# Loading the first image's shifted rows inside SBUF, in a convolution, attention and expert kernel

## What is computed

```python
xn = (x - mean) * rsqrt(var + 1e-5) * ln_g + ln_b          # mean, var over the whole image
Q, K, V = depthwise3x3(per_head_1x1(xn))                   # 8 heads of 24 channels
attn = softmax(K^T Q / alpha)                              # 24 x 24 per head, over channels
x = w_f (V attn) + b_f + xn
t = tokens(x)                                              # 1024 tokens of 192
t = t + proj(proj(causal_attention(layernorm(t))))         # 6 heads of 32; the projection is applied twice
t = t + experts(layernorm(t), top 2 of 4)                  # gelu, 192 -> 768 -> 192
```

## Time and profile before

| | us |
|---|---|
| median of 3 runs | 3337.73 |
| lowest and highest run | 3334.97, 3342.5 |
| span of the profiled execution | 3332.3 |
| TensorE busy | 3067.4 (92%) |
| first convolution round begins | 43.44 |
| fifth round (last pair's) begins | 79.19 |

### The profile page before, as it was taken

How to read it: one execution, slowest core, us unless ns; L and a number is a source line. 1 busy time by engine, 2 the same in 40 slices (tenths; PEclk the granted TensorE clock), 3 DMA queues, 4 the chain that set the end, 5 groups by cost and what they waited for, 6 DMA issues and landing times. The chain is left out here.

```text
span 3332.3 us, 72396 instructions
## 1 busy us (share of the span) xinstructions
PE 3067.4 (92%) x26642; PEld 2344.2 (70%) x26642; DVE 2202.3 (66%) x5619; ACT 1871.5 (56%) x3996; POOL 874.5 (26%) x1142
## 2 busy tenths in 40 slices
PE   4999999999999999999999999958999999999995
PEld 1666667666666676666766766637888888888884
DVE  3777677677776776777767767664555655655653
ACT  0647456465474664654746647535555555555553
POOL 2121313303223133132230331450223223223222
PEclk9999999999999999999999999979999999999997
DMA  7546445454364454544644546515667767667673
GB/s 177 142 114 178 115 124 148 124 150 126 113 184 116 122 149 122 153 118 120 173 125 115 148 123 154 156 47 159 195 206 213 221 208 220 210 205 228 206 212 120
DMA packets 256516, 519.82 MB, mean 156 GB/s; under 512 B 70919, under 2 KB 161991, under 8 KB 246521
## 3 DMA queue, kind: packets, MB, share of 16 engines
q1 hardware_dynamic: 222878, 453.58, 48.6%
q0 software_dynamic: 29184, 59.81, 6.0%
q10 hardware_dynamic: 4107, 1.81, 0.3%
HBM read 242.82 MB, written 117.71 MB: 108 GB/s over the span
## 5 line engine op out<-in xcount | busy, mean ns | idle before, releaser
L1051 DVE TENSOR_REDUCE minus_max<-ps 128x1 f32<-128x128 f32 (+7 forms) x768 | 571.6, 750 | 243.7 <-PE ps L1772 232.3
L1469 ACT ACTIVATE p_sb<-ps,minus_max 128x128 f32<-128x128 f32 (+7 forms) x768 | 569.3, 741 | 41.3 <-DVE minus_max L1051 37.8
L1782 PE MATMUL ps<-ident,p_sb 128*128 128x128 f32 x3456 | 530.6, 279 | 44.2 <-ACT p_sb L1469 18.4
L1356 DVE TENSOR_TENSOR g_lo<-g,g_hi 128x512 fp32r<-128x512 f32 x402 | 282.8, 704 | 369.3 <-ACT g_hi L1593 369.3
L1592 ACT ACTIVATE g<-ps,bcur 128x512 f32<-128x512 f32 x402 | 276.6, 688 | 429.2 <-PE ps L1967 429.2
L1483 ACT ACTIVATE PT<-ps 128x512 f32<-128x512 f32 (+3 forms) x768 | 396.7, 517 | 132.7 <-PE ps L1782 123.5
L1782 PEld LDWEIGHTS ps<-ident,p_sb 128*128 128x128 f32 x3456 | 370.0, 141 | 99.4 <-ACT p_sb L1469 37.5
L1983 PE MATMUL ps<-w_all,g_hi 128*128 x1608 | 434.6, 351 | 0.0
L1770 PE MATMUL ps<-KS,QS 96*128 96x512 f32 (+3 forms) x1152 | 393.6, 401 | 21.4 <-ACT p_sb L1469 17.9
L1647 PE MATMUL ps<-ring,wconv 125*32 125x512 f32 (+1 forms) x3072 | 358.4, 606 | 15.0 <-DMA ring<-padded_scratch 15.0
L780 POOL DMA_INDIRECT routed_rows<-xhat,slot x256 | 253.3, 989 | 358.2 <-issue 358.2
(11 more groups left out here) (276 smaller groups left out, 5442.5 us busy)
## 6 DMA issues: line engine op xcount, KB each, us to landing
ring<-padded_scratch SPq DMA_DIRECT2D x576, 204.0 KB
cur<-w_all SPq DMA_DIRECT2D x67, 1536.0 KB, 7.1
routed_rows<-zero_rows SPq DMA_DIRECT2D x67, 384.0 KB, 5.0
xgt<-routed_rows SPq DMA_DIRECT2D x67, 384.0 KB, 4.6
expert_rows<-y_rows SPq DMA_DIRECT2D x67, 384.0 KB, 3.0
padded_scratch<-xpad SPq DMA_DIRECT2D x32, 435.0 KB, 3.6
x_sb<-x SPq DMA_DIRECT2D x16, 768.0 KB, 5.5
KS<-QKh SPq DMA_DIRECT2D x128, 96.0 KB
```

Of the source, the lines that this page charges most:

```text
L1051: v.tensor_reduce(nmx[:, qc, h:h + 1], score_place(n), AX, ALU.max, negate=True).then_inc(mx_sb, 1)
L1356: v.tensor_tensor(g_lo[:, n % 2, :], g32[:, n % 2, :], g_hi[:, n % 2, :].bitcast(F32), ALU.subtract).then_inc(lo_sb, 1)
L1469: a.activation(p_sb[n % NP][:, 0:P * (qc + 1)], score_place(n), ACT.Exp, bias=nmx[:, qc, h:h + 1], accum_out=ls[:, qc, h:h + 1]).then_inc( ...
L1782: last = t.transpose(bank(pass_bank(piece))[:, P * k:P * (k + 1)], p_sb[n % NP][:, P * (k0 + k):P * (k0 + k + 1)], ident[:, :])
```

## The change

For the first image the ring is no longer filled through DRAM. `first_pair(sp, p)` waits for the half of xn that the pair lies in and issues 18 DMAs that copy 24 partitions each from `xpad` straight into `ring[p]`, so 72 DMAs of 102 KB in the place of two stores and 36 loads; SyncE issues the four pairs in order, right behind the mask rows. The semaphores `ring_ld[p]` count 288 for the first image and 144 for each later one. Before VectorE overwrites xpad for the second image it waits for the four pairs' copies, in the place of the stores. The seven gate loads go to ScalarE's queue, behind the projection's loads and ahead of the last small ones. TensorE runs `conv(0, 0)` first (after `setup_dve` 2, the product of L930), and the projection's products between `conv(0, 0)` and `conv(0, 1)`.

```diff
@@ -284,6 +284,7 @@
         setup_pool, inside_zero, mask_rows, setup_dve, setup_pe, w_split = sems(
             "setup_pool inside_zero mask_rows setup_dve setup_pe w_split")
         RING_LOADS = 16 * len(TAPS)
+        FIRST_LOADS = 2 * RING_LOADS
         STACK_LOADS = 16 * 3
         SENT = 16 * 2 * NC
 
@@ -324,6 +325,21 @@
                 sp.wait_ge(conv_ps, NR * i)
             sp.dma_start(x_sb[:, :, :], x[i].rearrange("(h p) a b -> p h (a b)", h=2)).then_inc(x_ld, 16)
 
+        def ring_loaded(i):
+
+            return FIRST_LOADS + RING_LOADS * i
+
+        def first_pair(queue, p):
+
+            half, at_row = p // 2, 2 * HC * (p % 2)
+            queue.wait_ge(xn_sb, half + 1)
+            for s, taps in enumerate(STACKS):
+                for j, tap in enumerate(taps):
+                    for h in range(2):
+                        rows = slice(at_row + HC * h, at_row + HC * (h + 1))
+                        queue.dma_start(ring[p][s][HC * j:HC * (j + 1), h, :],
+                                        xpad[rows, half, SHIFT[tap]:SHIFT[tap] + SL]).then_inc(ring_ld[p], 16)
+
         def write_scratch(sp, i, h):
 
             sp.wait_ge(xn_sb, 2 * i + h + 1)
@@ -331,7 +347,7 @@
 
         def load_pairs(sp, i, h):
 
-            sp.wait_ge(scr_w[h], 16 * (i + 1))
+            sp.wait_ge(scr_w[h], 16 * i)
             for p in (2 * h, 2 * h + 1):
                 for s, taps in enumerate(STACKS):
                     for j, tap in enumerate(taps):
@@ -510,17 +526,8 @@
                     sp.dma_start(ring[p][s][HC * nt:HC * nt + nt, :, :],
                                  inside_taps[taps[0]:taps[0] + nt, :].unsqueeze(1).to_broadcast([nt, 2, SL])
                                  ).then_inc(w_ld["mask"], 16)
-            write_scratch(sp, 0, 0)
-            load_pairs(sp, 0, 0)
-            write_scratch(sp, 0, 1)
-            sp.dma_start(gw_bc[:, 0:P, :], gate_w_a.partition_broadcast(P)).then_inc(w_ld["gate"], 16)
-            sp.dma_start(gw_bc[:, P:C, :], gate_w_b[0:CB, :].partition_broadcast(P)).then_inc(w_ld["gate"], 16)
-            sp.dma_start(bf_bc[:, 0:C], b_f.partition_broadcast(P)).then_inc(w_ld["gate"], 16)
-            sp.dma_start(gb_bc[:, :], gate_b.partition_broadcast(P)).then_inc(w_ld["gate"], 16)
-            sp.dma_start(gcol[:, :], gate_w_a[0:HALF, :]).then_inc(w_ld["gate"], 16)
-            sp.dma_start(ident_g[0:P - HALF, HALF:HALF + E], gate_w_a[HALF:P, :]).then_inc(w_ld["gate"], 16)
-            sp.dma_start(ident_g[P - HALF:HALF, HALF:HALF + E], gate_w_b[0:CB, :]).then_inc(w_ld["gate"], 16)
-            load_pairs(sp, 0, 1)
+            for p in range(PAIRS):
+                first_pair(sp, p)
             sp.dma_start(wqa_src[:, :], w_qkv_a).then_inc(w_ld["qkv"], 16)
             sp.dma_start(wqb_src[:, :], w_qkv_b).then_inc(w_ld["qkv"], 16)
             sp.wait_ge(setup_pool, 5)
@@ -905,8 +912,12 @@
                     if i:
 
                         dve.wait_ge(xn_flat, 2 * i)
+                        if i == 1:
+                            for p in range(PAIRS):
+                                dve.wait_ge(ring_ld[p], ring_loaded(0))
                         for h2 in range(2):
-                            dve.wait_ge(scr_w[h2], 16 * i)
+                            if i > 1:
+                                dve.wait_ge(scr_w[h2], 16 * (i - 1))
                 rows = lambda a: a.rearrange("p (a b) -> p a b", b=SW)
                 v.scalar_tensor_tensor(out=interior(h), in0=rows(x_sb[:, h, :]), scalar=img[:, 5:6],
                                        in1=rows(lnb[:, h, :]), op0=ALU.mult, op1=ALU.add).then_inc(xn_sb, 1)
@@ -1513,6 +1524,13 @@
             a.dma_start(bp_src[:, 0:1], b_proj[0:P].rearrange("(p a) -> p a", a=1)).then_inc(w_ld["proj"], 16)
             a.dma_start(bp_src[0:CB, 1:2], b_proj[P:C].rearrange("(p a) -> p a", a=1)).then_inc(w_ld["proj"], 16)
             a.dma_start(bpb[:, :], b_proj.partition_broadcast(P)).then_inc(w_ld["proj"], 16)
+            a.dma_start(gw_bc[:, 0:P, :], gate_w_a.partition_broadcast(P)).then_inc(w_ld["gate"], 16)
+            a.dma_start(gw_bc[:, P:C, :], gate_w_b[0:CB, :].partition_broadcast(P)).then_inc(w_ld["gate"], 16)
+            a.dma_start(bf_bc[:, 0:C], b_f.partition_broadcast(P)).then_inc(w_ld["gate"], 16)
+            a.dma_start(gb_bc[:, :], gate_b.partition_broadcast(P)).then_inc(w_ld["gate"], 16)
+            a.dma_start(gcol[:, :], gate_w_a[0:HALF, :]).then_inc(w_ld["gate"], 16)
+            a.dma_start(ident_g[0:P - HALF, HALF:HALF + E], gate_w_a[HALF:P, :]).then_inc(w_ld["gate"], 16)
+            a.dma_start(ident_g[P - HALF:HALF, HALF:HALF + E], gate_w_b[0:CB, :]).then_inc(w_ld["gate"], 16)
             for j in range(HPH):
                 a.dma_start(convb[W * j:W * j + HC, PAIRS:NR], conv_bias[2 * W:2 * W + HC, j:NH:HPH],
                             allow_slow_non_contiguous=True).then_inc(w_ld["small"], 16)
@@ -1612,25 +1630,14 @@
             pe.wait_ge(setup_pool, 2)
             average_mean(pe, 0, 4)
             average_var(pe, 0, 4)
-            pe.wait_ge(w_ld["proj"], 16 * 7)
-            pe.wait_ge(setup_dve, 4)
-            wa, wb, wta, wtb = wp_src[0], wp_src[1][0:CB, :], wp_src[2], wp_src[3][0:CB, :]
-            for b, rows, la, lb in ((5, P, wa[:, 0:P], wb[:, 0:P]), (6, CB, wa[:, P:C], wb[:, P:C]),
-                                    (7, P, bp_row[:, 0, :], bp_row[0:CB, 1, :])):
-                t.matmul(bank(b)[0:rows, 0:C], la, wta[:, :], start=True, stop=False, skip_group_check=True)
-                last = t.matmul(bank(b)[0:rows, 0:C], lb, wtb, start=False, stop=True, skip_group_check=True)
-                if rows == CB:
-                    t.matmul(bank(b)[CB:P, 0:C], la, wta[:, :], start=True, stop=False, skip_group_check=True)
-                    last = t.matmul(bank(b)[CB:P, 0:C], lb, wtb, start=False, stop=True, skip_group_check=True)
-            last.then_inc(setup_pe, 1)
-            pe.wait_ge(setup_dve, 4)
+            pe.wait_ge(setup_dve, 2)
             pe.wait_ge(w_ld["mask"], 16 * 2 * PAIRS)
             pe.wait_ge(img_veps, 1)
 
             def conv(i, r):
                 kind, n = ROUNDS[r]
                 if kind == "pair":
-                    pe.wait_ge(ring_ld[n], RING_LOADS * (i + 1))
+                    pe.wait_ge(ring_ld[n], ring_loaded(i))
                     tiles = [(2 * n + j % 2, W * (j // 2)) for j in range(4)]
                 else:
                     tiles = [(HPH * n + j, 2 * W) for j in range(4)]
@@ -1841,8 +1848,19 @@
                 t.matmul(o[:, E:2 * E], ones128[:, :], rowsum[:, :], start=True, stop=True, skip_group_check=True
                          ).then_inc(count_ps, 1)
 
-            for r in range(2):
-                conv(0, r)
+            conv(0, 0)
+            pe.wait_ge(w_ld["proj"], 16 * 7)
+            pe.wait_ge(setup_dve, 4)
+            wa, wb, wta, wtb = wp_src[0], wp_src[1][0:CB, :], wp_src[2], wp_src[3][0:CB, :]
+            for b, rows, la, lb in ((5, P, wa[:, 0:P], wb[:, 0:P]), (6, CB, wa[:, P:C], wb[:, P:C]),
+                                    (7, P, bp_row[:, 0, :], bp_row[0:CB, 1, :])):
+                t.matmul(bank(b)[0:rows, 0:C], la, wta[:, :], start=True, stop=False, skip_group_check=True)
+                last = t.matmul(bank(b)[0:rows, 0:C], lb, wtb, start=False, stop=True, skip_group_check=True)
+                if rows == CB:
+                    t.matmul(bank(b)[CB:P, 0:C], la, wta[:, :], start=True, stop=False, skip_group_check=True)
+                    last = t.matmul(bank(b)[CB:P, 0:C], lb, wtb, start=False, stop=True, skip_group_check=True)
+            last.then_inc(setup_pe, 1)
+            conv(0, 1)
             conv_transposes(0, 0)
             for i in range(B):
                 conv(i, 2)
```

## The result

The kernel with the change takes 3358.14 us (median of 7 runs, 3340.99 to 3369.21) against 3337.76 (7 runs, 3334.29 to 3342.5) of the kernel before: a ratio of 1.0052, with a 95% interval of 1.0037 to 1.0068. By the ratio it is slower by some 17 us; the two medians lie 20.4 us apart. The forecast was 3336 with a range of 3328 to 3345, so direction and range were both wrong. The profiled execution took 3360.47, with a span of 3358.6.

A forecast was written before the change was run, and what follows sets the result against it. TensorE, busy for 92% of the span, was taken as the bound, so only its start could move: 2 us off the span of 3332.3 gives 3330.3, plus 5.4 to the median gives 3336, range 3328 to 3345.

The forecast's parts named there:

- When the loads land: ScalarE's small loads in the first image's setup: `wf_t` expected at 50 to 58 us, hidden by the second pair.
- Late small loads: Rival: `wf_t` queued behind gate and projection loads beside the copies lands at 75, token rows at 107, 3345 us; chance 0.10.
- the prize: TensorE's 15.0 us of waiting for pairs; the waits on the store could give back some 8 us at most.
- The cost of an issue: SyncE's 72 copy issues at 0.43 us each, 7.8 us a pair, hidden under the 11.4 us transfer.
- The transfer: Copies inside SBUF filling the ring: 13.7 GB/s per busy engine, 0.317 us a row, 11.4 us a pair.
- The ratio of 1.22: A skill page's speedup of SBUF traffic over HBM traffic, giving 8.6 us a pair; the prediction said the trace disagrees.
- When they start: Copies issued at 18.95, held behind mask rows until about 26; pairs land at 41, 54, 65.6 and 77.2 us.
- The projection's products: TensorE's eight steps of 7.1 us, moved to 47.4 to 54.5, hidden by the second pair's wait but for 0.5 us.
- The rest: L930's product comes ten us before the first pair; VectorE's new wait and the dropped store wait cost or gain nothing.
- The sum's step: From the forecast span of 3330.3 to the median: 5.4 us added, giving 3335.7, say 3336.

The follow-up runs named there:

- e1: The kernel before with only the seven gate loads moved to ScalarE's queue, behind the projection's loads: 3341.03 us, ratio 1.0013.
- e6: The changed kernel with the last small loads (biases, alpha, `wf_t`) ahead of the projection's and gate's loads on ScalarE's queue: 3353.78 us, ratio 1.0054.
- e3: The changed kernel with SyncE holding the first copy until the projection's, gate and small loads have landed: 3353.24 us, ratio 1.0049.
- e4: The changed kernel with the projection's, gate, alpha and `wf_t` loads issued by SyncE ahead of the mask rows: 3336.82 us, ratio 0.9998.
- e7: The changed kernel with projection, alpha and `wf_t` loads early on SyncE, gate loads after pair 0, pairs 0 to 2 split between SyncE and ScalarE: 3341.47 us, 1.0014.
- e5: The kernel before with only the projection's products moved between the first and second convolution rounds: 3337.52 us, ratio 1.0002.
- e2: The kernel before with the SBUF copies alone, gate loads and projection's products left in their old places: 3349.39 us, ratio 1.0040.
- e9: The changed kernel with early projection, alpha and `wf_t` loads; SyncE copies pairs 0, 2, ScalarE pair 1 before its biases, pair 3 shared: 3347.67 us, 1.0025.

## Why the prediction was wrong

**When the loads land** is the step that failed, in the rival *Late small loads*. Its mechanism was the right one in kind; what was wrong was "I expect 50 to 58" and the chance of 0.10. The argument against it was "many small rows passed in between at the start (593 packets in 9 us)". That row was misread. Its window of the kernel before, 28 to 37, split where SyncE issues the first load of the ring, 28 to 28.86 and 28.86 to 37:

```profile
q10 hardware_dynamic: 297, 0.08, 45.7%
```

```profile
q1 hardware_dynamic: 348, 1.24, 67.6%
q10 hardware_dynamic: 296, 0.03, 3.9%
```

Half of the 593 packets passed in the first 0.86 us, before any load of the ring was issued. The other 296 took 8.1 us beside 348 of SyncE's; on 16 engines that is one per 0.44 us. This was already the slow turn-taking, and slower than the changed kernel's (546 in 10 us, one per 0.29). The rows of `wf_t`, which the prediction has "at nearly one for one", came slower than that: while they passed, from 38 to 44, ScalarE's queue passed 231 packets to 423 of SyncE's.

What had saved the loads before was the stretch just ahead, in which SyncE waited for its store and 1506 packets passed. The prediction read that wait as the prize. For ScalarE's loads it was the quiet in which they landed, and no step asked who else used it. One part the rival didn't have at all: it counted rows that wait in the queue, and 23.8 of the 33.3 us were lost earlier, in ScalarE's issuing. The gate loads alone account for 4.7 of these (e1 issues `wf_t` at 36.81).

The prediction said that "the projection's loads (another 44) have no quiet gap", but priced only `wf_t`. The products wait for these loads: 57.5 in place of the 47.4 at which they were put, and this alone moved the second round's end from 60.4 to 70.9. So a `wf_t` at 58 would not have saved the forecast: in e6 ScalarE is ready at 53.5, and the first transposes still begin at 77.7. And "from there to 99.84 it has about 30 us of work" was right as busy time (24.27 and 5.71 us from 78 to 124) but left out VectorE's waits: from its first piece to the token rows are 37.8 us before and 39.7 after. In the changed kernel it waits for TensorE's products 3.17 us until 89.32, 2.08 until 113.17, 2.87 until 117.54 and 1.48 until 123.28, the last three in the stretch at a granted clock of 0.50. Of the 16.3 us between the rival's 107 and the 123.3 measured, 6.6 lie ahead of the first piece (77 against 83.6) and 9.7 behind it.

**The cost of an issue** also failed: "SyncE's 72 issues cost 7.82 / 18 = 0.43 us each, 7.8 us a pair, under the 11.4 of its transfer, so they are hidden". Measured are 0.77, 13.8 a pair, above the transfer. The price of a load from DRAM was taken for a copy from SBUF; the trace of before had the nearer row, the key stacks' copies, whose issues take 607 ns in the median, 10.9 us a pair. That is just under the forecast transfer, so this row too would have called them hidden. In the changed kernel this cost nothing, since TensorE waited longer for other things; in e3 and e4 it set the pace.

**The transfer** held for one queue. 13.7 GB/s per engine and 0.317 us a row were forecast for the copies, and e3 shows 13.8 with nothing beside them. The ratio of 1.22 for traffic within SBUF, taken from the Trainium skill ("DMA: Bandwidth & Descriptors", section "Where 436 GB/s comes from"), doesn't show on one queue. From two, in e7, a busy engine moved 16.0 to 17.5 GB/s, 1.12 to 1.22 times the 14.3 of the loads.

**When they start** held nearly: the first pair was put at 41 and came at 42.95. This is in part luck, since the sum hid the issues behind the transfer. The pair's last copy was issued by about 32.1, so the pair landed some 10.9 us later; in e3, with nothing beside the copies, it landed 1.9 us after its last issue (52.1 and 53.94). How much of the 9 us between is due to the mask rows and how much to ScalarE's loads, no run tells. "Then 54, 65.6 and 77.2" can't be read from rounds that waited for something else; the last copy was issued at 72.8.

**The projection's products** cost nothing in their new place (e5), as forecast, as long as their loads are there. **The rest** held: the product of L930 (L941 after) came at 34.82, 5.5 us later than before and still ahead of the first pair. The sum's step of 5.4 us from span to median compares two executions: in the runs on record an execution is 1.7 to 3.4 us longer than its own span.

**The clock** was in no step. With the granted clock of 0.50 from 111.15 to 123.28 go 4.3 of the 23.4 us. e2, e7 and e9 have the same 12.1 us at 0.50 ahead of their token rows, each behind a wait of 3.2 us for VectorE's copy; e3 and e4 have 7.8 us at 1.00, behind a wait of 0.28. That the wait brings the lower clock wasn't tested.

## What to carry to other kernels

Before a wait is removed from a queue, list what other queues move in that stretch: their loads may land only because of it, and the wait then comes back at every engine that needs them. Loads that many things hang on belong ahead of the bulk transfer and not beside it; changing their order behind it only changes which is late. And an issue is to be priced by the nearest transfer of the same source and destination, since a DMA of 0.3 us a row can still be limited by the queue that issues it.

## What the chip showed that was not expected

A copy from SBUF to SBUF of 24 rows takes 714 ns to issue on SyncE and 736 on ScalarE (median of 27 in e7), a load of the same rows from DRAM 365. What in the source makes the difference was not settled.

Copies issued from two queues moved 215 GB/s at a share of 0.77, 17.5 GB/s per busy engine, against 13.8 from one queue; in the next two windows of e7, to 60 and to 70 us, it was 16.4 and 16.0. So the second queue didn't only fill the engines' pauses: each busy engine moved more.

ScalarE's own issuing slows beside the copies: one gate load took 3.42 us to issue at 29.52, and in e1, from the same queue but ahead of the ring's loads, 0.45 us at 26.85. That the queue holds the issue back because its loads can't pass fits this, but no run shows it.
